# An expert stage on one Trainium2 core: gelu over two PSUM banks at once, or bank by bank

## The reference

```python
scores = jnp.einsum('nsr,smr->nsm', z, C)
topv, topi = jax.lax.top_k(scores, K)
w = jax.nn.softmax(topv, axis=-1)
h = jax.nn.gelu(jnp.einsum('nsr,nskrh->nskh', z, W1g) + b1g)
yl = jnp.einsum('nskh,nskhr->nskr', h, W2g) + b2g
comb = jnp.einsum('nskr,nsk->nsr', yl, w)
out = jax.nn.gelu(comb @ G1 + g1b) @ G2 + g2b
```

## Time and profile before

| what | value |
|---|---|
| median of 3 runs | 1417.12 us (1416.96 to 1417.2) |
| profiled execution, its own time | 1417.62 us |
| its span, first to last instruction | 1415.6 us |
| mean granted TensorE clock | 0.943 of full speed |
| busy over the span: TensorE | 1238.1 us, 87% |
| VectorE | 1102.1 us, 78% |
| ScalarE | 1092.6 us, 77% |
| GpSimd | 1009.6 us, 71% |

### The profile page before, as it was taken

How to read it: one execution, slowest core, us unless ns; L and a number is a source line. 1 busy time by engine, 2 the same in 40 slices (tenths; PEclk the granted TensorE clock), 3 DMA queues, 4 the chain that set the end, 5 groups by cost and what they waited for, 6 DMA issues and landing times.

```text
span 1415.6 us, 34238 instructions
## 1 busy us (share of the span) xinstructions
PE 1238.1 (87%) x12232; PEld 621.1 (44%) x12232; DVE 1102.1 (78%) x3359; ACT 1092.6 (77%) x2707; POOL 1009.6 (71%) x735
## 2 busy tenths in 40 slices
PE   3842799999999999856999999999999999999996
PEld 3831465666666666522333333333333333333332
DVE  5574378889888988945888788888888888888884
ACT  0232556777677767437999999999999999999994
POOL 5661356765676566624887888888788888888894
PEclk7965799999999999967999999999999999999997
DMA  9554412222222222133124133222414323232410
GB/s 269 139 116 88 64 33 82 86 67 70 90 76 66 71 92 66 50 107 78 41 58 98 41 80 75 57 63 56 91 43 87 68 65 63 55 78 51 93 38 12
DMA packets 95704, 107.05 MB, mean 76 GB/s; under 512 B 12772, under 2 KB 92668, under 8 KB 95254
## 3 DMA queue, kind: packets, MB, share of 16 engines
q1 hardware_dynamic: 91184, 96.00, 26.5%
q10 hardware_dynamic: 2240, 5.08, 2.1%
q0 software_dynamic: 2112, 3.79, 1.1%
HBM read 67.88 MB, written 33.71 MB: 72 GB/s over the span
## 4 chain that ended last, share of the span: by engine, by line
ACT 24%; PE 19%; DVE 8%; issue 2%; POOL 1%; SPq 0%; DMA 0%; POOLq 0%; DVEq 0%; ACTq 0%
ACT ring L1047 16%; PE ring L1707 9%; PE code L1720 8%; ACT arena L1059 8%; DVE arena L1455 7%; PE ring L1739 2%; PE ring L1730 1%; ACT arena L1063 0%; POOL arena L801 0%; DMA bias_codes<-arena 0%; SPq L586 0%; SPq L591 0%; SPq L552 0%; ACT L1047 0%; POOLq L156 0%
## 5 line engine op out<-in xcount | busy, mean ns | idle before, releaser
L1455 DVE TENSOR_TENSOR arena<-ring,arena 128x496 f32<-128x496 f32 x1008 | 611.4, 667 | 142.9 <-ACT ring L1047 140.2
L801 POOL TENSOR_TENSOR arena<-arena 128x992 f32<-128x992 f32 x264 | 607.6, 2315 | 114.1 <-ACT arena L1059 104.2
L1047 ACT ACTIVATE ring<-ring 128x496 f32<-128x496 f32 x1008 | 545.2, 695 | 10.0 <-PE ring L1707 10.0
L1707 PE MATMUL ring<-arena,w_stack 99*32 99x496 bf16 x6144 | 430.8, 376 | 33.1 <-DVE arena L1455 27.4
L1720 PE MATMUL code<-arena,w_pad 128*32 128x496 f32 x3072 | 389.2, 581 | 3.7 <-ACT arena L1063 3.3
L1707 PEld LDWEIGHTS ring<-arena,w_stack 99*32 99x32 bf16 x6144 | 160.0, 95 | 423.7 <-DVE arena L1455 259.2
L1059 ACT ACTIVATE arena<-ring 128x992 f32<-128x992 f32 x252 | 283.9, 1127 | 3.1 <-POOL arena L801 3.1
L1549 PE MATMUL ring<-arena 96*128 96x372 f32 x384 | 135.3, 490 | 1.6 <-ACT arena L904 0.9
L1720 PEld LDWEIGHTS code<-arena,w_pad 128*32 128x32 f32 x3072 | 96.7, 110 | 54.1 <-DVE arena L1455 17.9
L739 POOL TENSOR_TENSOR arena<-arena 128x372 f32<-128x372 f32 x96 | 91.1, 975 | 35.2 <-DVE arena L1295 35.2
L1549 PEld LDWEIGHTS ring<-arena 96*128 96x128 f32 x384 | 71.8, 194 | 62.4 <-ACT arena L912 15.8
(11 more groups left out here) (139 smaller groups left out, 1460.7 us busy)
## 6 DMA issues: line engine op xcount, KB each, us to landing
arena<-gates SPq DMA_DIRECT2D x48, 496.0 KB, 6.7
gates<-arena SPq DMA_DIRECT2D x16, 744.0 KB, 11.6
arena<-h_scratch SPq DMA_DIRECT2D x32, 279.0 KB
arena<-z_parts SPq DMA_DIRECT2D x144, 62.0 KB, 2.7
h_scratch<-arena SPq DMA_DIRECT2D x16, 279.0 KB
z_parts<-arena SPq DMA_DIRECT2D x48, 93.0 KB, 2.1
arena<-h_scratch SPq DMA_DIRECT2D x12, 372.0 KB
out_h<-arena SPq DMA_DIRECT2D x12, 372.0 KB
```

The source lines that it names most:

```text
L801: p_.tensor_tensor(gated[:, quad % SPACES, j:j + 2], hid[:, POOL_DUOS.index(duo) % 2], gst[:, block // EB, j:j + 2], ALU.mult).then_inc(s_ ...
L1047: a_.activation(product, product, ACT.Gelu_apprx_tanh).then_inc(s_hid, 1)
L1455: v_.tensor_tensor(gated[:, quad % SPACES, j + p], duo_bank(duo, p), gst[:, block // EB, j + p], ALU.mult).then_inc(s_gat, 1)
L1707: mm = t_.matmul(bank[32 * q:32 * q + 32], w1s[:, x + 32 * q:x + 32 * q + 32], zst[:, o, j + p], start=True, stop=True)
```

## The change

In the expert stage, ScalarE's gelu for GpSimd's pairs is split into two narrow instructions, one per bank, for all 22 pairs of a tile. Each waits for the product of its own bank alone. The wait for the SBUF buffer (`s_pg`) now stands ahead of both. Each gelu signals `s_hid`, so that the semaphore counts banks for all pairs, and `banks_gelu` gets simple. TensorE's `bank_free` asks for the bank's own gelu instead of the pair's. GpSimd still asks for the second one of the pair (`piece=1` by default) and multiplies both banks in one instruction. The value of what is computed does not change.

```diff
 def banks_gelu(tile, duo, piece=1):
-    full = len(POOL_DUOS) + 2 * len(DVE_DUOS)
-    before = sum(1 if d in POOL_DUOS else 2 for d in range(duo))
-    return full * tile + before + (1 + piece if duo in DVE_DUOS else 1)
+    return 2 * (DUOS * tile + duo) + piece + 1
...
             def gelu(tile, duo):
-                if duo in DVE_DUOS:
-                    for k in range(2):
-                        act.wait_ge(s_hp1, 2 * (DUOS * tile + duo) + k + 1)
-                        product = duo_bank(duo, k)
-                        a_.activation(product, product, ACT.Gelu_apprx_tanh).then_inc(s_hid, 1)
-                    return
-                act.wait_ge(s_hp1, 2 * (DUOS * tile + duo + 1))
-                to_pool = hid[:, POOL_DUOS.index(duo) % 2]
-                wait(act, s_pg, pool_gated(tile, duo) - 2)
-                if duo in WRAPS:
-                    for k in range(2):
-                        product = duo_bank(duo, k)
-                        last = a_.activation(to_pool[:, k], product, ACT.Gelu_apprx_tanh)
-                    last.then_inc(s_hid, 1)
-                else:
-                    product = duo_banks(duo)
-                    a_.activation(to_pool, product, ACT.Gelu_apprx_tanh).then_inc(s_hid, 1)
+                to_pool = hid[:, POOL_DUOS.index(duo) % 2] if duo in POOL_DUOS else None
+                if duo in POOL_DUOS:
+                    wait(act, s_pg, pool_gated(tile, duo) - 2)
+                for k in range(2):
+                    act.wait_ge(s_hp1, 2 * (DUOS * tile + duo) + k + 1)
+                    product = duo_bank(duo, k)
+                    a_.activation(product if to_pool is None else to_pool[:, k], product,
+                                  ACT.Gelu_apprx_tanh).then_inc(s_hid, 1)
...
                 elif user in POOL_DUOS:
-                    wait(pe, s_hid, banks_gelu(before, user))
+                    wait(pe, s_hid, banks_gelu(before, user, piece))
```

## The result

The changed kernel takes 1428.94 us (median of 3 runs, 1428.54 to 1428.96) against 1417.12: slower, by a ratio of 1.0074 with a 95% interval of 1.0053 to 1.0096. The forecast was 1428.9, in a range of 1424.5 to 1433. The profiled execution took 1428.54, 10.92 more than that of before.

The account below looks back on a forecast made before the run. ScalarE was taken to be full in the expert stage; 21 splits in tile 0 plus 11 x 16 made 197 paid at 0.06 us, 11.8 us, on 1417.12: 1428.9 us, range 1424.5 to 1433.

Parts of the forecast that it names:

- The bound: Expert stage: ScalarE is full, so the spacing of its gelus' ends, not their durations, tells what is paid.
- The price of a split: Each wide gelu made two narrow ones costs ScalarE 0.06 us: 0.96 for pair 40 against 0.90 for a wide one.
- whole-latency rival: ScalarE pays full durations for each split, 0.26 us each: 51 us in all, 1468 us; chance 0.02.
- Which are paid: All 21 splits in tile 0 and 16 of 21 in each of 11 other tiles: 197 paid, 11.8 us.
- the 16: Splits paid per tile after the first: pairs 4, 7, 9, 20, 23, 26 and the ten from 34 to 62.
- five are free: Pairs 12, 15, 18, 29 and 31: their splits are swallowed by ScalarE's stalls in every tile but the first.
- Stalls B and C: ScalarE's waits for TensorE near the two output products, 0.40 and 0.70 us per tile; each to shrink about 0.06.
- Stall A: ScalarE's wait for GpSimd before pair 20, 0.40 us per tile; to shrink by about 0.18.
- what costs nothing: Second signal, second wait, the buffer wait placed ahead and TensorE's earlier first bank: no cost and no gain.
- the step before it: GpSimd starts pair 9 0.14 us after that pair's gelu ends, so it moves back and pair 9's split is paid.
- The way by VectorE: Pair 26's split delays VectorE's multiplications, so TensorE's second output product: paid, though ScalarE gets it back at a stall.
- The end: GpSimd's last pair, then code and output, follow the gelu of pair 62: nothing of the 11.8 us is lost.

Follow-up runs that it names:

- e1: Kernel before with GpSimd's pairs split into two narrow gelus, but both waits ahead and one signal behind: 1431.34 us, ratio 1.0081, tiles of 63.34 us.
- e8: Changed kernel with each narrow gelu of GpSimd's pairs cut into two halves of a bank, no more waits or signals: 1455.65 us, ratio 1.0257.
- e9: Kernel before with seven of VectorE's pairs (6, 36, 39, 44, 50, 55, 58) given one wide gelu: 1415.87 us, ratio 0.9965.
- e11: Kernel before with sixteen VectorE pairs made wide, those with neighbouring banks from 5 to 8 and 36 to 58: 1410.3 us, ratio 0.9938.
- e6: Kernel before with 33 of VectorE's pairs, those whose banks are neighbours, given one wide gelu: 1430.84 us, ratio 1.0076.
- e3: Kernel before with all GpSimd pairs but 12, 15, 18, 29 and 31 split, a signal per bank: 1430.48 us, ratio 1.0075, tiles of 63.32 us.
- e2: Kernel before with only GpSimd pairs 12, 15, 18, 29 and 31 split, a signal per bank: 1419.69 us, ratio 0.9998, tiles of 62.40 us.
- e5: Kernel before, gelus still wide, with ScalarE's wait for GpSimd's buffer placed ahead of its wait for the products: 1419.2 us, ratio 0.9997.

## Why the prediction was right

**The bound.** ScalarE was full, and its end spacing was the right measure. e1, e8 and e9 show it from three sides: starts added without a signal cost time, two more starts a pair cost 0.13 where one had cost 0.06, starts taken away gave time.

**The price of a split.** Taken as 0.06 from pair 40's two rows; the changed kernel shows 0.97 for a pair against 0.90, 0.06 to 0.07. The durations would have said 0.26 and the whole-latency rival 1468; they fail by a factor of four. The Trainium skill's "Perfetto Trace Analysis", section "Optimizing Scalar/DVE Operations", says that larger operations can improve throughput where the engine is saturated. The change and e9 to e11 agree (0.06 us for a start on a full ScalarE); e6 does not, for there larger operations made ScalarE wait.

**Which are paid.** Tile 0 and pairs 4 and 7 grew by 1.45 us for 23 splits, 0.063 each: all paid. Per tile 0.915 instead of the 0.96 forecast: the cost is that of the 16, as e3 shows (63.32 with those alone), and five are free, as e2 shows. Stalls B and C shrank by 0.05 and 0.07, forecast 0.06 each. Stall A shrank by 0.27 by the rows, not by 0.18.

**The step that was short** is one sentence of "what costs nothing": that the place of ScalarE's wait for the buffer does not matter. It does, a little: of the 16, pair 20 cost nothing in the end. GpSimd's pair 15 ended at 1040.10 in the kernel before (first row below, the timeline of GpSimd), and pair 20 started 0.10 later; in the changed kernel it ended at 1045.51 and pair 20 started at 1045.54.

```profile
1037.78 2.32 POOL L801 TENSOR_TENSOR arena<-arena 128x992 f32<-128x992 f32 x1
```

The changed kernel, with the gelu of pair 9 and GpSimd's multiplications of pairs 9 and 15, from the timelines of ScalarE and GpSimd:

```profile
1034.77 1.18 ACT L1047 ACTIVATE arena<-ring 128x496 f32<-128x496 f32 x2
...
1036.09 2.32 POOL L799 TENSOR_TENSOR arena<-arena 128x992 f32<-128x992 f32 x1
...
1043.19 2.32 POOL L799 TENSOR_TENSOR arena<-arena 128x992 f32<-128x992 f32 x1
```

So from the end of pair 9's gelu to that of pair 20 the changed kernel takes 10.65 us (1035.95 to 1046.60), where the kernel before took 10.66 (1030.54 to 1041.20): the earlier restart made up for the split of pair 20. e1, with the old order, shows it as paid, in tiles 0.04 us longer. e5 shows that the order alone shortens the restart, and also that this need not shorten the tile. The first two rows of the changed kernel confirm the step before it: GpSimd starts pair 9 at 1036.09, 0.14 after its gelu's end at 1035.95, so that pair 9 is paid through GpSimd.

**The way by VectorE** is as forecast in the rows too (timelines of VectorE and TensorE, beside the earlier trace rows): the multiplications end at 1056.31 and the second output product starts at 1056.36. TensorE's own work ahead of it had ended at 1056.29, so it was VectorE that the product waited for; before, no such gap stood there.

```profile
1055.06 1.25 DVE L1444 TENSOR_TENSOR arena<-ring,arena 128x496 f32<-128x496 f32 x2
...
1055.27 1.02 PE L1696 MATMUL ring<-arena,w_stack 99*32 99x496 bf16 x16
1056.36 0.91 PE L1728 MATMUL ring<-g2w,arena 65*124 65x192 f32 x4
```

**The end.** The stage's 11.43 us against 11.8 is mainly the 0.06 at stall A in each of eleven tiles, some 0.7 in all, partly made up by a price slightly above 0.06. That the medians differ by 11.82 owes something to luck: the profiles differ by 10.92, with 0.70 of that from stages that no edit touches.

## What to carry to other kernels

Where an engine is full, cost an edit by the spacing of its ends, not by mean durations, and look for a place in the same trace where the new form already runs. Then follow each added piece to the next stall and ask what the awaited engine itself hangs on: a stall that hangs on the slowed engine gives nothing back. Split work bank by bank only where somebody waits for the first bank; here VectorE's pairs need it in some places, GpSimd's gained nothing from it, and wide gelus for sixteen of VectorE's pairs were faster than either kernel.

## What was not expected of the hardware

ScalarE's restart after a wait depends on which of two waits is written last: 0.10 us after GpSimd's end with the unfinished wait second (before, e1), 0.03 to 0.04 with it first (after, e5).

The durations of ScalarE's rows grow while it runs without a stall, a wide gelu from 1.25 to 1.38 us within 8 us, while the spacing of the ends stays. In e8 the single gelu for the tile before took up 0.30 us of that growth. So an instruction without idle time ahead of it can still hold slack.

A wait can also stand in the rows without idle time. In the kernel before, pair 18 writes the buffer that GpSimd's pair 12 reads, and starts at 1037.92, 0.09 us after GpSimd's end at 1037.83; but for rounding that is the lag of pair 20 behind pair 15. No idle time is shown there, since the rows of the gelus ahead of it reach beyond its start. The list of waits has only the one for pair 20.

```profile
1035.52 2.31 POOL L801 TENSOR_TENSOR arena<-arena 128x992 f32<-128x992 f32 x1
...
1037.92 1.04 ACT L1059 ACTIVATE arena<-ring 128x992 f32<-128x992 f32 x1
```
